# Delta attention's last inverse corner is closed one wave later, beside the next wave's product, and the recurrence runs two waves behind

## What is computed

```python
q = q * rsqrt(dk)
g_cum = cumsum(g)
decay = exp(tril(g_cum[:, None] - g_cum[None, :]))
L = -(k_beta @ k.T) * decay                      # strictly lower
attn = solve_triangular(eye - L, eye, lower=True)  # the inverse
v_intra = attn @ v_beta
k_cumdecay = attn @ (k_beta * exp(g_cum))
def scan_body(state, x):                         # chunk after chunk
    a_i = tril(q_i @ k_i.T * decay_i)
    v_new = v_i - k_cumdecay_i @ state
    out_i = (q_i * exp(g_i)) @ state + a_i @ v_new
    new_state = state * exp(g_last) + (k_i * exp(g_last - g_i)).T @ v_new
xf = core * silu(z); xf = xf * rsqrt(mean(xf * xf) + EPS) * norm_weight
return xf @ W_out
```

## Time and profile before

| what | us |
|---|---|
| three runs | 2058.67, 2054.18, 2058.14 |
| median of the runs | 2058.14 |
| the profiled execution | 2054.93 |
| its span, first to last instruction | 2053.1 |
| outside the span | 1.8 |

### The profile page before, as it was taken

One profiled execution on the slowest core, in us unless ns is written; L12 is line 12 of the kernel. 1 busy time (PEld: TensorE's weight loads), 2 busy tenths in 40 slices (PEclk: granted clock), 3 DMA queues, 4 the chain that ended last, 5 costly groups with the idle time before them and its releaser, 6 DMA issues.

```text
span 2053.1 us, 45861 instructions
## 1 busy us (share of the span) xinstructions
PE 1850.3 (90%) x16855; PEld 1191.3 (58%) x16855; DVE 1287.1 (63%) x2490; ACT 995.4 (48%) x2433; POOL 1072.0 (52%) x2252
## 2 busy tenths in 40 slices
PE   7799997867898885898999999999999999999987
PEld 5422664422244453445677777777777777677766
DVE  2544564685577422535777777777777777777753
ACT  2375232215321341434566656655665666566653
POOL 0521222323100302033888888887888878888873
PEclk7899999989999796899999999999999999999999
DMA  6044422200001333101222222222222222222221
GB/s 155 1 121 148 109 46 56 72 34 1 20 25 26 96 106 95 34 19 40 53 55 61 55 52 63 63 54 53 63 63 54 53 58 63 53 53 62 44 53 33
DMA packets 229260, 121.36 MB, mean 59 GB/s; under 512 B 141712, under 2 KB 208816, under 8 KB 228784
## 3 DMA queue, kind: packets, MB, share of 16 engines
q1 hardware_dynamic: 223424, 109.06, 21.3%
q0 software_dynamic: 5616, 9.38, 2.2%
HBM read 84.88 MB, written 36.68 MB: 59 GB/s over the span
## 4 chain that ended last, share of the span: by engine, by line
PE 22%; POOL 20%; issue 6%; SPq 3%; DVE 3%; DMA 3%; ACT 2%; POOLq 0%; DVEq 0%; ACTq 0%
POOL a_term L2594 8%; POOL a_z L2598 8%; PE ps L2046 5%; PE ps L2056 3%; PE ps L2245 3%; SPq L1979 2%; POOL a_rstd L2570 2%; POOL a_xnorm L2576 2%; DMA a_l<-a_v_dram 2%; PE ps L2276 2%; SPq L1987 1%; DVE a_v L2653 1%; PE ps L2212 1%; PE ps L2286 1%; PE ps L2221 1%
## 5 line engine op out<-in xcount | busy, mean ns | idle before, releaser
L2594 POOL TENSOR_TENSOR a_term<-a_z,a_l 32x14 f32<-32x14 f32 (+6 forms) x896 | 342.1, 382 | 70.3
L2598 POOL TENSOR_TENSOR a_z<-a_z,a_term 32x14 f32<-32x14 f32 (+6 forms) x896 | 341.7, 381 | 70.2
L2624 DVE SCALAR_TENSOR_TENSOR a_qkv<-a_raw,a_taps,a_qkv 128x1024 f32<-128x1024 f32 x192 | 247.0, 1286 | 6.1
L2046 PE MATMUL ps<-all_xn,a_w_qkv 128*128 128x512 f32 x512 | 246.9, 608 | 0.0
L388 POOL DMA_INDIRECT f_rows<-a_row,a_slots x32 | 35.7, 1116 | 192.1 <-DVE a_of_tile L377 146.7
L2245 PE MATMUL ps<-a_out_t,a_w_out 128*128 128x256 f32 x512 | 129.1, 395 | 1.9 <-ACT a_out_t L2468 1.7
L2046 PEld LDWEIGHTS ps<-all_xn,a_w_qkv 128*128 128x128 f32 x512 | 89.1, 193 | 69.3 <-issue 67.5
L2389 ACT ACTIVATE a_raw<-ps 128x512 f32<-128x512 f32 x128 | 76.3, 598 | 108.7 <-PE ps L2046 108.0
L2056 PE MATMUL ps<-a_w_z,all_xn 128*128 128x256 f32 x512 | 122.6, 383 | 0.0
L849 POOL DMA_INDIRECT f_sums<-a_y,a_xs x23 | 36.0, 1566 | 136.5 <-ACT a_y L798 133.5
L2588 POOL COPY a_z<-a_l 32x256 f32<-32x256 f32 x64 | 27.4, 429 | 152.3 <-DMA a_l<-a_v_dram 152.0
(11 more groups left out here) (331 smaller groups left out, 4303.7 us busy)
## 6 DMA issues: line engine op xcount, KB each, us to landing
a_gc_rows<-a_g_dram SPq DMA_DIRECT2D x64, 256.0 KB, 4.7
a_v_dram<-a_v SPq DMA_DIRECT2D x64, 256.0 KB
a_w<-in_f_w SPq DMA_DIRECT2D x24, 512.0 KB, 4.5
a_w_qkv<-in_a_w SPq DMA_DIRECT2D x16, 512.0 KB, 3.8
a_t_dram<-a_z SPq DMA_DIRECT2D x512, 8.0 KB
a_xs<-f_rows SPq DMA_DIRECT2D x46, 130.0 KB, 2.2
a_w_z<-in_a_w SPq DMA_DIRECT2D x16, 256.0 KB, 2.8
a_w_out<-in_a_wo SPq DMA_DIRECT2D x16, 256.0 KB, 3.1
```

The costliest lines, as they stand in the source:

```text
L2046: mm = pe.matmul(ps[:, to, :], w_qkv[:, k, mt * P:(mt + 1) * P], xn[:, k, b * T:(b + 1) * T], start=k == 0, stop=k == KC - 1)
L2594: pool.tensor_tensor(term[:, 0:j, j + 1:], z[:, 0:j, j:j + 1].broadcast_to([HP, j, n]), rows[:, j:j + 1, j + 1:].broadcast_to([HP, j, n]), ...
L2598: pool.tensor_tensor(z[:, 0:j, j + 1:], z[:, 0:j, j + 1:], term[:, 0:j, j + 1:], ALU.add).then_inc(sub_step, 1)
L2624: dve.scalar_tensor_tensor(to, rows, tap, to, ALU.mult, ALU.add).then_inc(conv_ready if j == TAPS - 1 else conv_step, 1)
```

## The change

- **The last corner.** The product of `close_c` is taken out of iteration w and done in iteration w + 1. `join_and_close_c(w)` issues the four products that begin the corner of wave w and the four that close the corner of wave w - 1 alternately, one of each per problem. The first read partitions 0 to 63 and write PSUM partitions 64 to 127, the others the reverse, both into the upper half of bank BW. They share an SBUF buffer `corner`, whose upper partitions hold what `t_half` held and whose lower ones what `wc` held.
- **The copies.** `copy_whole` (ACT, 128x512) is gone. DVE's `copy_z_half` becomes `copy_halves`: two copies of 64 partitions, which put the two diagonal halves into `inv`; ACT's `copy_closed` (64x256) puts the corner there. The fourth quarter of `inv` is filled with zeros once.
- **The recurrence** of a wave, and all that follows it, moves one iteration later on every engine: `w - 1` becomes `w - 2`, `w - 2` becomes `w - 3`. `at` and `qg` get 5 buffers instead of 4, and the loops run one iteration longer.
- **ACT's order.** `copy_wc` moves behind part 2 and, in iterations with c = 1, behind the third SiLU; `copy_closed` stands right after it.
- **z's order** of tiles (`Z_ORDER`), and a wait for `xf_ready` before the third and fourth `silu_z`. SP loads `w_out` in iterations with c = 3 instead of 2.

```diff
-                def join_c(w):
-                    pe.wait_ge(th_ready, w + 1)
+                def join_and_close_c(w):
+                    if made(w):
+                        pe.wait_ge(th_ready, w + 1)
+                    if made(w - 1):
+                        pe.wait_ge(wc_ready, w)
+                        pe.wait_ge(zh_ready, w)
+                    if made(w - 2):
+                        pe.wait_ge(inv_ready, w - 1)
                     for r in range(PR):
-                        mm = pe.matmul(upper(BW)[SECOND, r, :], v0[FIRST, w % 3, r, SECOND], t_half[FIRST, r, :],
-                                       start=True, stop=True)
-                    mm.then_inc(wc_psum, 1)
-                def close_c(w):
-                    pe.wait_ge(wc_ready, w + 1)
-                    pe.wait_ge(zh_ready, w + 1)
-                    for r in range(PR):
-                        mm = pe.matmul(bank(BZ)[FIRST, r, SECOND], wc[SECOND, r, :], z_half[SECOND, r, :],
-                                       start=True, stop=True)
-                    mm.then_inc(c_psum, 1)
+                        if made(w):
+                            begun = pe.matmul(upper(BW)[SECOND, r, :], v0[FIRST, w % 3, r, SECOND],
+                                              corner[FIRST, r, :], start=True, stop=True)
+                        if made(w - 1):
+                            closed = pe.matmul(upper(BW)[FIRST, r, :], corner[SECOND, r, :],
+                                               inv[SECOND, (w - 1) % 2, r, SECOND], start=True, stop=True)
...
-                for w in range(W + 2):
-                    if made(w - 1):
-                        recall(w - 1)
+                for w in range(W + 3):
+                    if made(w - 2):
+                        recall(w - 2)
...
                     if made(w):
-                        join_c(w)
-                    if made(w - 2):
-                        project_out(w - 2)
+                        join_and_close_c(w)
+                    if made(w - 3):
+                        project_out(w - 3)
                     part(w, 3)
-                    if made(w):
-                        close_c(w)
...
-                def copy_z_half(w):
+                def copy_halves(w):
                     dve.wait_ge(b_psum, w + 1)
-                    dve.tensor_copy(z_half[SECOND, :, :], bank(BZ)[SECOND, :, SECOND]).then_inc(zh_ready, 1)
+                    if w >= 2:
+                        dve.wait_ge(x_psum, w - 1)
+                    for of in (SECOND, FIRST):
+                        cp = dve.tensor_copy(inv[of, w % 2, :, of], bank(BZ)[of, :, of])
+                    cp.then_inc(zh_ready, 1)
```

More of the change, by code:

```diff
@@ L2198, in ask @@
                 def ask(w):
+                    if w == 1:
+                        pe.wait_ge(xf_ready, 1)
                     if w >= 2:
@@ L2205, in ask @@
                     for r in range(PR):
-                        pe.matmul(bank(BO)[:, r, :], qg[:, w % 4, r, :], state[:, r, :], start=r == 0, stop=False)
+                        pe.matmul(bank(BO)[:, r, :], qg[:, w % 5, r, :], state[:, r, :], start=r == 0, stop=False)
                 def answer(w):
@@ L2392, in silu_z @@
                     act.wait_ge(z_ready, 4 * g + n + 1)
-                    act.activation(zs[:, g % 2, 2 * n:2 * n + 2, :].rearrange("p t n -> p (t n)"),
+                    if g >= 2 and n >= 2:
+                        act.wait_ge(xf_ready, CH * (g - 1))
+                    first = 2 * Z_ORDER[n]
+                    act.activation(zs[:, g % 2, first:first + 2, :].rearrange("p t n -> p (t n)"),
                                    ps[:, of, :], ACT.Silu).then_inc(zs_ready, 1)
@@ L2602, in substitute @@
                                      z16[:, w % 2, 0, :].rearrange("p (c i) -> p i c", c=SB)).then_inc(sub_done, 1)
-                for w in range(-2, W + 1):
+                for w in range(-2, W + 2):
                     if made(w + 2):
                         substitute(w + 2)
-                    if made(w - 1):
-                        root(w - 1)
-                        normed(w - 1)
+                    if made(w - 2):
+                        root(w - 2)
+                        normed(w - 2)
             @block.vector
@@ L2843, in _ @@
                     if made(w):
-                        copy_z_half(w)
+                        copy_halves(w)
                     if not late:
```

98 lines of the change are left out of this document (56 added, 42 removed).

## The result

The changed kernel takes 2069.52 us (median of 8 runs, 2062.64 to 2072.62), the kernel before 2059.24 in runs of the same chips (8 runs, 2054.05 to 2065.91): 1.0044 times, 95% interval 1.0024 to 1.0064. A second comparison gives 1.0024 [1.0007, 1.0041]. The change costs some 5 to 10 us; 2059 was forecast, and the measured time is above the range. Of the new kernel's 8 runs the profiled one is the lowest, 2062.64 us; its span is 2060.8, against 2053.1 before. The trace explains these 7.7 us; the 3 or so more by which the medians differ in this first comparison it does not. Part of such scatter lies outside the change: the stage with the change begins, at the first `join_a`, between 937.2 and 950.9 us in the fourteen traces of this document, though the change edits next to nothing that runs before it.

The account below looks back on a forecast made before the run. PE looked like the bound, with POOL, a loop through c = 1 and DVE nearly level; after the change PE no longer. Heads -5 and ends +6.4 gave +1.4 on the 2058.14 median: 2059 us, range 2045 to 2068.

Parts of the forecast that it names:

- The pairs: Closing and beginning corner products on PE overlap fully: about 0.65 us together, 0.60 us less per wave, 2.4 per head.
- The chain through c = 1 up to the scores: From `xf` with c = 0 through `solve` (waiting about 1 us for `rest`) and `turn_out` at 17.6 to scores at 25.1 us.
- Rival 2: Slower: DVE and PE with c = 1 become the bound, at `solve` behind `rest`; 2066 to 2075 us; chance 0.17.
- From the scores on nothing changes: From the scores to the next `xf` with c = 0, the times stay 10.19, 16.78 and 16.98 us.
- the term -0.35 per head: Each head 0.35 us shorter: 0.15 from the chain to the scores, 0.2 from shorter PE; -5 us over 14 full heads.
- The end: One more iteration with nothing beside it costs 10.7 us; the three iterations before it lose 0.60 each.
- The -1.8: The three iterations before the extra one lose 0.60 us each, since PE waits for little but itself there.
- The start: Iteration 1 has no recurrence and POOL follows at once: 2.5 us saved, bounds 0 and 3.5.
- The last rival: The pairs run without overlap, PE is back at 67.5 us per head, a head at 69.9: 2064.5 us; chance 0.10.

Follow-up runs that it names:

- f1_rest_first: The changed kernel with DVE making `rest` ahead of `low` in iterations with c = 1: 2064.17 us, 1.0023 times the kernel before.
- the repeat: The changed kernel measured once more, unchanged, against the kernel before: 2064.24 us, 1.0024 times.
- the swap: The kernel before with ACT's last SiLU of z ahead of the copy of the inverse where c = 1: 2046.20 us (0.9946), again 2052.39 us (0.9964).

## Why the prediction was wrong, step by step

- **The pairs: right.** 0.62 us for both products against 0.65 forecast, 4.49 us of idle PE per head against 4.5. Sixteen instructions of two row tiles, into different partitions of bank BW, pass in 0.62 us; eight alone took 0.63. The Trainium skill, page "TensorEngine Tiling (Array Packing)", section "Restrictions and Gotchas", says that different row tiles cannot access the same PSUM bank simultaneously; as a rule on time the trace does not bear it out here.
- **The chain through c = 1 up to the scores: right.** 17.33 us to `turn_out` (17.6), 24.93 to the scores (25.1), the wait for `rest` 0.76 (about 1). But with the wait taken away, in `f1_rest_first`, the head gained nothing: `turn_out` then waited for POOL. The working was right in its numbers and left out that POOL's steps move with DVE's order. (Rival 2's "each copy pays its own semaphore" is a misreading of the kernel: only the second copy signals.)
- **"From the scores on nothing changes": wrong, and so is the term -0.35 per head. This is the step that failed.** The prediction charged the second copy once, on DVE in one iteration, and took POOL's steps as fixed at 16.4 to 16.8 us. They are not: over a head the four take 67.59 us instead of 66.80 (67.45 in the repeat), because DVE's convolution meets POOL's instructions at another point, and this took back what POOL waits less. In the loop's columns it is 0.24 us (0.28) from the substitution of c0 to `normed`. From scores to substitution the loop lost another 0.28 (0.46). The head gave -0.1 instead of -0.35; from the join of wave 2 to that of wave 58, 14 heads, it is -1.0 us instead of -5. Why the blocks land later is open: L itself ends as long after the scores as before, 4.11 us against 4.15, and the last of the blocks' DMAs is issued 5.01 us after L's end instead of 4.69, nearly all of it between the first and the last of the four DMAs that read the blocks back (1.55 us instead of 1.25). Every kernel that closes a wave late or lags shows 10.70 to 11.06 there, every one that does not and keeps `recall` first 10.44 to 10.56.
- **The end: one term right, one wrong.** The extra iteration costs 10.3 us (10.7 forecast). The end as a whole, from the last `join_a`, costs +9.5. The -1.8 in the three iterations before it never came: 69.5 us from the join of wave 58 to that of 63 before, 69.4 after (71.1 in the repeat). The term took PE as the bound there, and PE's relief did not show.
- **The start: wrong, -2.5 forecast, 0 measured.** From the join of wave 0 to that of wave 2 it is 31.6 us before and 31.9 after. Iteration 1 has less work on PE, and PE waits instead: 3.63 us for the widened blocks and 1.71 for the last SiLU of z, where before it waited 1.63 and 0.50. The bound of 0 was in my own range for this term; I took the value near the other end, on the argument that POOL follows at once, for which I had no row.
- **Sum.** Forecast -5 - 1.8 - 2.5 + 10.7 = +1.4; the trace has -0.9 for all up to the last `join_a` and +9.5 behind it, +8.7 with rounding for the stage; the stage begins 1 us earlier in this execution, hence +7.7 for the span. Against the forecast the stage is 7.3 us long: 4.0 from the 14 heads, 2.8 from the start and 1.7 from the iterations before the end, less 1.2 at the end. The -1.8, the -2.5 and 0.2 of the 0.35 per head were booked against PE's being the bound, after I had written that it no longer was. The bounds of the ends were added up wrongly too: with the terms' own bounds they are 10.7 - 1.8 - 3.5 = +5.4 and +10.7, not +4 and +11. The last rival, pairs that don't overlap, is refuted by the rows above; that its 2064.5 is near the repeat is chance.
- **The range** missed the first median by 1.5 us; the repeat, 2064.24, lies in it. It ended near 2068, and took in neither that all gains could fail together nor that one comparison differs from the next by 0.2%. That the repeat lies in it is no merit of the working, since three of its terms failed there as well.

## What to carry to other kernels

When several engines are nearly level, cut one period of the kernel into a loop that crosses them and compare its pieces between traces: an engine 97% busy gave back 2.2 us per head and the head shortened by 0.1. Deepening a software pipeline by one iteration costs a full unaccompanied iteration at the end, here 10 us, so ask first which single piece of the change shortens the loop; here it was the order of two instructions on ACT, which needs no deeper pipeline. Price a copy on an engine with idle time by what is queued behind it. And do not take a step of an engine as fixed when another engine stretches its instructions: here 15.9 of POOL's 66.8 us per head, before the change, are time beyond the shortest of each instruction, nearly all of it beside a DVE instruction, and moving DVE's work by 0.4 us moved that sum by 0.8.

## What was unexpected of the hardware

- **POOL stops beside DVE's convolution.** A POOL instruction of 0.25 us takes 1.25 beside a `scalar_tensor_tensor` of DVE of 1.28 us that reads two fp32 tensors from SBUF, and only 0.22 beside a DVE copy out of PSUM. DVE pays nothing: of its 174 such steps in the stage none is longer than 1.35 us before, and only one after (1.42). The Trainium skill, page "SBUF — State Buffer", section "Who interferes with whom", says that a DVE instruction with two SBUF inputs contends with a GpSimd instruction that reads SBUF, that the port pair the two share is an exclusive lock, and that issue order decides who blocks; the trace agrees that the POOL instruction goes on only when the step is over (1787.32 + 1.43 is 1788.75; the step started at 1787.38 and takes 1.28). By the recorded starts POOL came first here, by 0.06 us, and was held all the same; starts on POOL are too rough to settle that. The first step of the convolution, a `tensor_scalar` of 0.74 us, stretches one as well, from some 0.2 us to 0.69. How late the row of POOL instructions meets the convolution is worth up to a third of a microsecond per wave.
- **Two groups of 64x64 products overlap** also when written one after the other: 0.89 us for both, against 0.62 alternated and 1.23 in different places.
- **Half the clock for a part of z (3.78 us against 1.99) cost nothing that shows**: PE waited 3.63 us in front of it and 1.71 behind it, and with the clock kept up the two iterations took as long.
- **The repeat differs.** The same pair of kernels gave 1.0044 and 1.0024, and the swap 0.9946 and 0.9964; a difference of two or three tenths of a per cent was taken above only together with one in the pieces of the loop.
